# Sparse mixture-of-experts block: weight low halves moved between GpSimd and VectorE

## The chip, the cores and the metric

One core of a Trainium2 chip runs the whole kernel in one launch. The metric is device time in microseconds (us) of that core. Its engines run their own instruction lists side by side and meet only at semaphores: TensorE (PE in the profile), VectorE (DVE), ScalarE (ACT), GpSimd (POOL) and SyncE (SP, which here only issues DMAs).

## The reference, cut to what matters

```python
x = x + tanh(g_xattn) * xattn(layernorm(x), ctx, mask)      # (2, 1024, 256) tokens x width
h = layernorm(x)                                            # 2048 tokens
top_logits, top_idx = top_k(h @ w_router, 2)                # 8 experts, two for each token
moe = sum over the two chosen experts e of
      score_e * ((silu(proj_e) * gate_e) @ fc2_w[e])        # proj_e, gate_e = split(h @ fc1_w[e])
shared = (silu(h @ gate_w) * (h @ up_w)) @ down_w           # 512 wide, for every token
x = x + tanh(g_ffn) * (moe + shared)
```

## The kernel before, in words

All matmuls that need full float32 accuracy are done in three passes: each operand is split into a high half (the value rounded to the matmul's type) and a low half (what is left). For the weights, ScalarE writes the high halves (`cut_hi`) and `cut_lo` writes the low halves as `raw - high`, one 128x512 chunk at a time, on GpSimd or on VectorE. There are 30 chunks: 0 to 5 belong to the shared part, 6 to 29 to the experts (three for each). The split by engine is by hand: `by_pool(i)` is true for the chunks before `IN_A` (7), for those in `MID` and for those in `LAST` (27, 28, 29); these are GpSimd's. All others are VectorE's.

The stages that matter here, in order of time:

1. The shared part of the FFN runs on TensorE in 16 units (4 groups of 512 tokens by 4 slices of 128). From unit 4 on, `gate_up_down(n, n - 2)` interleaves gate and up of unit n with the down product of unit n - 2. VectorE serves each unit with `product(n)` (L690 or L692), then `cut_later(n)`, which cuts `LATER[n]` of VectorE's own chunks (L243), then `product_lo(n)` (L630), the low half of the unit's activations. The down product of unit n needs `product_lo(n)`. Units 14 and 15 are held back for the end of the kernel.
2. Meanwhile GpSimd scatters the 2048 normalised token rows to the two experts of each, into the DRAM buffer `rows`: 32 indirect DMAs of 128 rows (L388), 16 for each half of the tokens, `scatter(h, n0, n1)`. The low halves of `MID` stand between them by hand, those of `LAST` behind the last scatter.
3. When all scatters have landed, SyncE loads the 39 expert tiles of 128 rows each (`hrows<-rows`, L281). TensorE transposes tile 0 (L1245), does `down(12)`, transposes tile 1, and waits for all weight low halves before the first expert matmul `m_up(0)` (L994).
4. The loop over the 39 tiles, then the two units held back, and the sums.

TensorE's own order at the seam of stages 1 and 3 is `gate_up(13)`, `down(11)`, `m_turn_x(0)`, `down(12)`, `m_turn_x(1)`, `m_up(0)`. `down(n)` and `product_lo(n)` meet at this wait:

```python
            def down(n):
                g, f = n // FC, n % FC
                after(pe, "chunk_lp", SCH)
                after(pe, "act_l", n + 1)
```

On VectorE the same place reads `product(12)`, three low halves, `product_lo(12)`, `product(13)`, `m_x(0)`.

Of the kernel before, what the change touches and what calls it, by code (L numbers as in the profile page):

```python
# [44 lines left out]
HT = NT // NH  # L45
IN_A = 7
HELD = 2
U0 = UNITS - HELD
MID = tuple(IN_A + 2 * i for i in range(5))
LAST = tuple(range(CHUNKS - 3, CHUNKS))  # L50
LATER = {3: 1, 4: 1, 5: 1, 6: 1, 7: 1, 8: 1, 9: 2, 10: 2, 11: 2, 12: 3}
ORDER = list(range(SCH + 8)) + list(range(SCH + 12, CHUNKS)) + list(range(SCH + 8, SCH + 12))


def build(nc, x, ctx_t, ctx_in, mask, small, W_t, chunks, out):
# [6 lines left out]
    with ExitStack() as ctx:  # L62
# [149 lines left out]
        def after(eng, name, value):  # L212
            if not (isinstance(value, int) and value <= 0):
                eng.wait_ge(s[name], value)
# [13 lines left out]
        def chunk_bufs(i):  # L228
            c = ORDER[i]
            raw_, hi_, lo_ = (sw_raw, sw_hi, sw_lo) if c < SCH else (ew_raw, ew_hi, ew_lo)  # L230
            c = c if c < SCH else c - SCH
            return raw_[:, c, :], hi_[:, c, :], lo_[:, c, :]

        def by_pool(i):
            return i < IN_A or i in MID + LAST

# [3 lines left out]
        def cut_lo(eng, i):  # L240
            after(eng, "chunk_h", i + 1)
            raw_, hi_, lo_ = chunk_bufs(i)
            eng.tensor_tensor(out=lo_, in0=raw_, in1=hi_.bitcast(F32), op=ALU.subtract)\  # L243
                .then_inc(s["chunk_lp" if by_pool(i) else "chunk_lv"], 1)
# [60 lines left out]
        def _(pool):  # L305
# [64 lines left out]
            def weight_fields(h):  # L370
                sl = slice(HT * h, HT * h + HT)
                after(pool, "tg_half", 2)
                after(pool, "w_tanh", h + 1)
                pool.tensor_scalar(hrows[:, sl, D + 2], wsm[:, 3, sl], tgh[:, 0:1], tgh[:, 0:1], ALU.mult, ALU.add)\
                    .then_inc(s["fields"], 1)
                pool.tensor_scalar(hrows[:, sl, D + 3], wsm[:, 3, sl], tgh[:, 1:2], None, ALU.mult)\
                    .then_inc(s["fields"], 1)

            def scatter(h, n0, n1):
                if n0 == 0:  # L380
                    after(pool, "h_ready", HT * (h + 1))
                    after(pool, "fields", 2 * (h + 1))
                    after(pool, "low_expert", h + 1)
                    after(pool, "const_r", 6)
                    after(pool, "slots", h + 1)
                for n in range(n0, n1):
                    k, i = n % 2, n // 2
                    pool.indirect_dma_start(  # L388
                        out=rows, out_offset=bass.IndirectOffsetOnAxis(ap=slot[:, h, k, i:i + 1], axis=0),
                        in_=hrows[:, HT * h + i, :], in_offset=None, bounds_check=PAD_ROW - 1, oob_is_err=False,  # L390
                    ).then_inc(s["scattered"], 16)
# [20 lines left out]
            rstd_second(NG - 1)  # L412
            scatter(0, 3, 8)
            cut_lo(pool, MID[0])
            scatter(0, 8, 12)
            cut_lo(pool, MID[1])
            scatter(0, 12, 2 * HT)
            cut_lo(pool, MID[2])
            weight_fields(1)
            scatter(1, 0, 6)  # L420
            cut_lo(pool, MID[3])
            scatter(1, 6, 11)
            cut_lo(pool, MID[4])
            scatter(1, 11, 2 * HT)
            for i in LAST:
                cut_lo(pool, i)
            for t in range(N_TILES):
# [198 lines left out]
        def _(v):  # L626
# [163 lines left out]
            def cut_later(u):  # L790
                mine = [i for i in range(IN_A, CHUNKS) if i not in MID + LAST]
                first = sum(m for w, m in LATER.items() if w < u)
                for i in mine[first:first + LATER.get(u, 0)]:
                    cut_lo(v, i)
# [557 lines left out]
```

## Time and profile before

| what | value |
|---|---|
| median of 3 runs | 240.39 us |
| the three runs | 238.53, 250.59 and 240.39 us |
| span of the profiled execution, first to last instruction | 237.5 us |
| TensorE busy in it | 222.3 us (94%) |
| VectorE busy | 171.8 us (72%) |
| GpSimd busy | 125.1 us (53%) |
| ScalarE busy | 129.8 us (55%) |
| granted TensorE clock, mean | 0.998 |

The total time of the profiled execution is not given apart from its span; the quickest of the three runs is 1.03 us longer than the span. Busy shares are averages over all stages. The kernel's stages have different limits, so the rows below are taken from the stretch from 70 to 122 us, in which the scatters run and the expert tiles begin.

### The profile page before, as it was taken

To read this page: it belongs to the slowest core of one execution; us is meant where nothing else is said; L and a number is where in the kernel's file an instruction comes from. 1 tells how busy PE (TensorE), PEld (TensorE's weight loads), DVE (VectorE), ACT (ScalarE), POOL (GpSimd) and SP (SyncE) were. 2 spreads that over 40 slices of the span, in tenths; PEclk is the share of its full clock that TensorE was granted. 3 is DMA by queue.
4 is the path that set the end of the run, shared out by engine and by line. 5 is a ranking of instruction groups with operands and counts; after the bars stand their busy time and mean duration, and the time that the engine had idled before them with its cause. 6 is when DMAs were issued, how large, how long until landed. Compare 5 with 4: busy or idle time off the path is not lost.

```text
span 237.5 us, 5283 instructions
## 1 busy us (share of the span) xinstructions
PE 222.3 (94%) x1425; PEld 193.7 (82%) x1425; DVE 171.8 (72%) x513; ACT 129.8 (55%) x316; POOL 125.1 (53%) x177
## 2 busy tenths in 40 slices
PE   7688999999989999999599999999999999999984
PEld 7578999978778888888488888888888888888763
DVE  0977897797767799999977665665665665664794
ACT  2465788773647645464125656656656656655320
POOL 1688898464777887887701334334334334334600
PEclk9999999999999999999999999999999999999999
DMA  5999950000121225322242443343343332008877
GB/s 154 286 362 406 404 199 3 0 0 25 45 94 67 74 85 179 136 91 92 67 123 65 135 127 94 96 125 96 88 127 92 94 120 68 37 38 267 288 238 310
DMA packets 18131, 32.05 MB, mean 135 GB/s; under 512 B 3046, under 2 KB 9323, under 8 KB 18104
## 3 DMA queue, kind: packets, MB, share of 16 engines
q1 hardware_dynamic: 14096, 22.28, 29.8%
q0 software_dynamic: 3408, 8.46, 9.5%
q10 hardware_dynamic: 600, 0.97, 1.3%
q8 instruction: 13, 0.21, 0.4%
q14 instruction: 14, 0.11, 0.2%
HBM read 19.95 MB, written 12.67 MB: 137 GB/s over the span
## 4 chain that ended last, share of the span: by engine, by line
PE 46%; POOL 8%; issue 6%; DMA 2%; DVE 2%; SPq 0%; DVEq 0%; ACT 0%; POOLq 0%
PE bank L994 38%; POOL rows L388 6%; PE bank L1245 4%; PE bank L1265 3%; POOL ew_lo L243 2%; DMA rows<-hrows,slot 1%; DMA hrows<-rows 1%; DVE act_lo L630 1%; DVE acc L710 0%; PE bank L1179 0%; DVE act L929 0%; DVE acc L966 0%; SPq L280 0%; ACT act L581 0%; DVEq L62 0%
## 5 line engine op out<-in xcount | busy, mean ns | idle before, releaser
L430 POOL DMA_INDIRECT parts<-y_out,dst x39 | 38.7, 991 | 69.9 <-DVE dst L923 66.1
L388 POOL DMA_INDIRECT rows<-hrows,slot x32 | 35.0, 1095 | 12.3 <-issue 12.3
L929 DVE TENSOR_TENSOR act<-act,bank 128x256 f32<-128x256 f32 x39 | 16.4, 421 | 34.5 <-issue 25.0
L581 ACT ACTIVATE act<-bank 128x256 f32<-128x256 f32 x39 | 15.0, 384 | 37.1 <-PE bank L994 37.1
L994 PE MATMUL bank<-ew_hi,m_xt_hi 128*128 x78 | 30.9, 396 | 0.1
L994 PE MATMUL bank<-ew_hi,m_xt_lo 128*128 x78 | 30.8, 395 | 0.0
L994 PE MATMUL bank<-ew_lo,m_xt_hi 128*128 x78 | 30.7, 394 | 0.0
L994 PE MATMUL bank<-ew_hi,act_hi 128*128 x78 | 25.2, 323 | 0.1
L994 PE MATMUL bank<-ew_hi,act_lo 128*128 x78 | 21.9, 281 | 0.0
L994 PE MATMUL bank<-ew_lo,act_hi 128*128 x78 | 21.9, 281 | 0.0
L443 ACT ACTIVATE act_hi<-act 128x512 fp32r<-128x512 f32 x16 | 10.1, 630 | 21.2 <-DVE act L690 9.1
L593 ACT ACTIVATE y_out<-bank,w_t 128x256 f32<-128x256 f32 x39 | 18.5, 475 | 4.0 <-PE bank L994 1.1
L443 ACT ACTIVATE m_xt_hi<-bank 128x256 fp32r<-128x256 f32 x39 | 14.9, 381 | 5.8 <-PE bank L1245 5.8
L630 DVE TENSOR_TENSOR act_lo<-bank,act_hi 128x256 fp32r<-128x256 f32 x39 | 16.5, 423 | 1.6 <-ACT act_hi L443 1.0
L994 PEld LDWEIGHTS bank<-ew_hi,m_xt_lo 128*128 128x128 f32 x78 | 14.7, 188 | 3.3
L1245 PEld LDWEIGHTS bank<-ident,hrows 128*128 128x128 f32 x78 | 10.7, 140 | 8.0 <-issue 3.1
L1245 PE MATMUL bank<-ident,hrows 128*128 128x128 f32 x78 | 14.9, 272 | 2.5 <-DMA hrows<-rows 2.5
L994 PEld LDWEIGHTS bank<-ew_hi,m_xt_hi 128*128 128x128 f32 x78 | 14.7, 188 | 2.2 <-issue 0.4
L630 DVE TENSOR_TENSOR m_xt_lo<-bank,m_xt_hi 128x256 fp32r<-128x256 f32 x39 | 16.1, 414 | 0.4 <-ACT m_xt_hi L443 0.4
L443 ACT ACTIVATE act_hi<-bank 128x256 fp32r<-128x256 f32 x39 | 15.0, 384 | 2.6 <-PE bank L1265 0.6
L994 PEld LDWEIGHTS bank<-ew_lo,m_xt_hi 128*128 128x128 f32 x78 | 14.7, 188 | 1.8
L243 DVE TENSOR_TENSOR ew_lo<-ew_raw,ew_hi 128x512 fp32r<-128x512 f32 x15 | 15.6, 1037 | 0.2
(186 smaller groups left out, 655.6 us busy)
## 6 DMA issues: line engine op xcount, KB each, us to landing
ew_raw<-in_chunks SPq DMA_DIRECT2D x12, 512.0 KB, 10.7
hrows<-rows SPq DMA_DIRECT2D x39, 130.0 KB, 2.1
low_buf<-parts SPq DMA_DIRECT2D x4, 512.0 KB, 4.6
high_buf<-parts SPq DMA_DIRECT2D x4, 512.0 KB, 3.9
acc<-in_x SPq DMA_DIRECT2D x7, 256.0 KB, 4.6
sw_raw<-in_chunks SPq DMA_DIRECT2D x3, 512.0 KB, 9.0
out<-acc SPq DMA_DIRECT2D x3, 512.0 KB, 3.0
rows<-pad_rows SPq DMA_DIRECT2D x9, 130.0 KB
```

Source lines behind the costliest of these rows:

```text
L243: eng.tensor_tensor(out=lo_, in0=raw_, in1=hi_.bitcast(F32), op=ALU.subtract)\
L388: pool.indirect_dma_start(out=rows, out_offset=bass.IndirectOffsetOnAxis(ap=slot[:, h, k, i:i + 1], axis=0), in_=hrows[:, HT * h + i, :], ...
L430: pool.indirect_dma_start(out=parts, out_offset=bass.IndirectOffsetOnAxis(ap=dst[:, t:t + 1], axis=0), in_=y_out[:, t % SLOTS, :], in_offs ...
L443: return a.activation(out_, in_, ACT.Identity).then_inc(s[name], 1)
L581: a.activation(act[:, p, 0:I], M_H[p][:, 0:I], ACT.Silu).then_inc(s["m_sil"], 1)
L593: a.activation(y_out[:, t % SLOTS, :], M_Y[p][:, 0:D], ACT.Identity, scale=w_t[:, t:t + 1])\
L630: return TT(out_, in_, hi_.bitcast(F32), ALU.subtract).then_inc(s[name], 1)
L929: TT(act[:, p, 0:I], act[:, p, 0:I], M_H[p][:, I:2 * I], ALU.mult).then_inc(s["m_prod"], 1)
L994: ins = pe.matmul(ps, a, b, start=first and i == 0, stop=last and i == total - 1, skip_group_check=not lone)
L1245: ins = pe.transpose(M_X[:, k * P:(k + 1) * P], hrows[:, i, k * P:(k + 1) * P], ident[:])
L1265: ins = pe.transpose(M_A[:, k * P:(k + 1) * P], act[:, p, k * P:(k + 1) * P], ident[:])
```

## The change

Chunks 9 and 15 go from GpSimd to VectorE. The scatters, which stood in series of 5, 4, 4, 6, 5 and 5 between the low halves of the list, now stand in series of 5, 8, 8 and 8. VectorE's list of chunks gets chunk 9 in unit 4 and chunk 15 (by its place in the list, 16 and 17 stand there) in unit 8: each of the two units cuts one more.

```diff
-MID = tuple(IN_A + 2 * i for i in range(5))
+MID = (IN_A, IN_A + 4, IN_A + 6)
-LATER = {3: 1, 4: 1, 5: 1, 6: 1, 7: 1, 8: 1, 9: 2, 10: 2, 11: 2, 12: 3}
+LATER = {3: 1, 4: 2, 5: 1, 6: 1, 7: 1, 8: 2, 9: 2, 10: 2, 11: 2, 12: 3}
@@ on GpSimd
             cut_lo(pool, MID[0])
-            scatter(0, 8, 12)
+            scatter(0, 8, 2 * HT)
             cut_lo(pool, MID[1])
-            scatter(0, 12, 2 * HT)
+            weight_fields(1)
+            scatter(1, 0, 8)
             cut_lo(pool, MID[2])
-            weight_fields(1)
-            scatter(1, 0, 6)
-            cut_lo(pool, MID[3])
-            scatter(1, 6, 11)
-            cut_lo(pool, MID[4])
-            scatter(1, 11, 2 * HT)
+            scatter(1, 8, 2 * HT)
             for i in LAST:
                 cut_lo(pool, i)
```

GpSimd before, from the fourth scatter of the first half of the tokens to its last low half; L388 is a scatter, L243 a low half, L374 and L376 write the routing weights of the second half:

```order
L388 DMA rows<-hrows,slot 17536x260 x5
L243 TENSOR_TENSOR ew_lo<-ew_raw,ew_hi 128x512
L388 DMA rows<-hrows,slot 17536x260 x4
L243 TENSOR_TENSOR ew_lo<-ew_raw,ew_hi 128x512
L388 DMA rows<-hrows,slot 17536x260 x4
L243 TENSOR_TENSOR ew_lo<-ew_raw,ew_hi 128x512
L374 TENSOR_SCALAR hrows<-wsm,tgh 128x8
L376 TENSOR_SCALAR hrows<-wsm,tgh 128x8
L388 DMA rows<-hrows,slot 17536x260 x6
L243 TENSOR_TENSOR ew_lo<-ew_raw,ew_hi 128x512
L388 DMA rows<-hrows,slot 17536x260 x5
L243 TENSOR_TENSOR ew_lo<-ew_raw,ew_hi 128x512
```

Behind these, five more scatters and the three low halves of `LAST` follow. The same place in the changed kernel:

```order
L388 DMA rows<-hrows,slot 17536x260 x5
L243 TENSOR_TENSOR ew_lo<-ew_raw,ew_hi 128x512
L388 DMA rows<-hrows,slot 17536x260 x8
L243 TENSOR_TENSOR ew_lo<-ew_raw,ew_hi 128x512
L374 TENSOR_SCALAR hrows<-wsm,tgh 128x8
L376 TENSOR_SCALAR hrows<-wsm,tgh 128x8
L388 DMA rows<-hrows,slot 17536x260 x8
L243 TENSOR_TENSOR ew_lo<-ew_raw,ew_hi 128x512
L388 DMA rows<-hrows,slot 17536x260 x8
L243 TENSOR_TENSOR ew_lo<-ew_raw,ew_hi 128x512 x3
```

Two low halves are gone from between the scatters, and nothing else on GpSimd has changed its order.

VectorE before, in unit 8: `product(8)`, its low half of weights, `product_lo(8)`, `product(9)`:

```order
L904 CAST t_off<-t_offf 128x39
L690 TENSOR_TENSOR act<-act,bank 128x512
L243 TENSOR_TENSOR ew_lo<-ew_raw,ew_hi 128x512
L630 TENSOR_TENSOR act_lo<-act,act_hi 128x512
L690 TENSOR_TENSOR act<-act,bank 128x512
```

And in the changed kernel, whose lines are numbered four lower from here on:

```order
L900 CAST t_off<-t_offf 128x39
L686 TENSOR_TENSOR act<-act,bank 128x512
L243 TENSOR_TENSOR ew_lo<-ew_raw,ew_hi 128x512 x2
L626 TENSOR_TENSOR act_lo<-act,act_hi 128x512
L686 TENSOR_TENSOR act<-act,bank 128x512
```

One low half more stands ahead of the activations' low half. The other added one stands in unit 4, behind `product(4)` and ahead of the slots of the second half (`place`, L783 before). The orders of TensorE, ScalarE and SyncE are the same.

## Rows read from the trace of the kernel before

**Rows 1.** The page, part 1: busy us (share of the span) xinstructions

```profile
PE 222.3 (94%) x1425; PEld 193.7 (82%) x1425; DVE 171.8 (72%) x513; ACT 129.8 (55%) x316; POOL 125.1 (53%) x177
```

**Rows 2.** The chain of waits at the seam: start us, us, what

```profile
111.64 0.30 issue
111.95 2.90 DMA rows<-hrows,slot
...
115.66 2.14 DMA hrows<-rows
117.79 0.14 issue
117.93 0.41 PE bank L1245 x2
118.34 0.17 issue
118.51 1.67 PE bank L994 x12
```

**Rows 3.** GpSimd's timeline: start us, us, instruction [idle before <-releaser]

```profile
73.51 1.00 POOL L388 DMA_INDIRECT rows<-hrows,slot  x1 [0.16 <-issue]
...
76.14 0.97 POOL L388 DMA_INDIRECT rows<-hrows,slot  x1 [0.30 <-issue]
77.41 1.30 POOL L388 DMA_INDIRECT rows<-hrows,slot  x1 [0.31 <-issue]
78.72 1.31 POOL L243 TENSOR_TENSOR ew_lo<-ew_raw,ew_hi 128x512 fp32r<-128x512 f32 x1
80.20 0.99 POOL L388 DMA_INDIRECT rows<-hrows,slot  x1 [0.17 <-issue]
...
87.96 1.08 POOL L388 DMA_INDIRECT rows<-hrows,slot  x1 [0.85 <-issue]
...
93.55 1.49 POOL L388 DMA_INDIRECT rows<-hrows,slot  x1 [0.30 <-issue]
95.35 0.97 POOL L388 DMA_INDIRECT rows<-hrows,slot  x1 [0.30 <-issue]
96.34 1.30 POOL L243 TENSOR_TENSOR ew_lo<-ew_raw,ew_hi 128x512 fp32r<-128x512 f32 x1
...
104.81 1.32 POOL L243 TENSOR_TENSOR ew_lo<-ew_raw,ew_hi 128x512 fp32r<-128x512 f32 x1
...
111.95 1.39 POOL L388 DMA_INDIRECT rows<-hrows,slot  x1 [0.30 <-issue]
113.35 3.77 POOL L243 TENSOR_TENSOR ew_lo<-ew_raw,ew_hi 128x512 fp32r<-128x512 f32 x3
```

**Rows 4.** GpSimd's groups, 86 to 114 us: xcount | busy us, mean ns | idle before

```profile
L388 POOL DMA_INDIRECT rows<-hrows,slot x16 | 18.4, 1152 | 5.1 <-issue 5.1
```

**Rows 5.** VectorE's timeline, 77 to 119 us

```profile
77.18 0.68 DVE L243 TENSOR_TENSOR ew_lo<-ew_raw,ew_hi 128x512 fp32r<-128x512 f32 x1
79.42 0.23 DVE L783 TENSOR_TENSOR place<-bank,e_reg 128x64 f32<-128x64 f32 x1 [1.55 <-PE bank L1091]
...
96.50 1.19 DVE L904 CAST t_off<-t_offf 128x39 int32<-128x39 f32 x1
...
99.04 0.69 DVE L630 TENSOR_TENSOR act_lo<-act,act_hi 128x512 fp32r<-128x512 f32 x1 [0.15 <-issue]
...
104.47 2.95 DVE L243 TENSOR_TENSOR ew_lo<-ew_raw,ew_hi 128x512 fp32r<-128x512 f32 x2
...
111.14 0.75 DVE L692 SCALAR_TENSOR_TENSOR act<-act,tg,bank 128x512 f32<-128x512 f32 x1 [0.35 <-PE bank L1144]
111.81 5.87 DVE L243 TENSOR_TENSOR ew_lo<-ew_raw,ew_hi 128x512 fp32r<-128x512 f32 x3
117.71 0.69 DVE L630 TENSOR_TENSOR act_lo<-act,act_hi 128x512 fp32r<-128x512 f32 x1
```

**Rows 6.** TensorE's timeline: unit 10 begins, and the seam

```profile
99.88 0.41 PE L1144 MATMUL bank<-ht_hi,sw_hi 128*128 128x512 f32 x1
...
115.19 0.28 PE L994 MATMUL bank<-sw_hi,act_lo 128*128 128x256 f32 x1
117.93 0.41 PE L1245 MATMUL bank<-ident,hrows 128*128 128x128 f32 x2 [2.46 <-DMA hrows<-rows]
```

## The prediction

> **What bounds the kernel now.** I read the busy shares first: TensorE is busy 94% of the span [rows 1], so a change on GpSimd and VectorE can only pay where TensorE waits. The chain of waits then names the place. From about 84 us to 112 us it runs over GpSimd's scatters, then over the landing of the last scatter, the load of the first expert tile and its transpose [rows 2]. TensorE's timeline shows what that costs: the last matmul of `down(11)` ends at 115.47 us, and the transpose of tile 0 starts at 117.93, an idle time of 2.46 us ended by the tile's load [rows 6]. That is all this seam can give back at the transposes, however early the scatters end.
>
> The reader should look at one more line of the chain: between the transposes (end 118.34) and `down(12)` (start 118.51) there are 0.17 us put down to nothing [rows 2]. `down(12)` needs `product_lo(12)`, and on VectorE this one runs from 117.71 to 118.40 [rows 5]. So two things come last together: the tile's load and VectorE's low half of activations. The chain shows only the first. Why VectorE is so late stands in its timeline: the three weight low halves of unit 12 take 5.87 us [rows 5], while one low half takes 0.68 [rows 5]. The excess, 5.87 - 3 x 0.70 = 3.77 us, is exactly the time of GpSimd's three `LAST` low halves, 113.35 to 117.12 [rows 3]. VectorE's third low half ends at 117.68, 0.56 us behind GpSimd's end. The same is seen at 104.47, where two of VectorE's take 2.95 us beside one of GpSimd's from 104.81 to 106.13, and at 96.50, where a small cast takes 1.19 us and ends 0.05 us behind GpSimd's low half [rows 3, 5]. `product(12)` reads PSUM and took a plain 0.75 us, but nothing in that row is a test, since GpSimd was at a scatter then. In this trace GpSimd's low half runs its 1.3 us whatever VectorE does, and VectorE's operation on SBUF waits for it.
>
> **Part 1: two low halves leave GpSimd's list.** Scatters in a quiet stretch start 1.27 us apart (76.14 to 77.41) [rows 3]. With a low half between, it costs its own 1.31 us plus 0.17 of gap behind it, and saves the 0.30 gap between two scatters: 1.31 + 0.17 - 0.30 = 1.18 us. Two of them: 2.36 us off the path that ends at 113.35.
>
> **Part 2: what the moved work does to the scatters.** A scatter beside VectorE work is often longer than its 0.97: the 16 of the second half of the tokens take 18.4 us [rows 4], 18.4 - 16 x 0.97 = 2.9 us over. Single ones are 1.30 beside a VectorE low half at 77.18, 1.39 beside those at 111.81, 1.49 at 93.55 [rows 3, 5]. One more VectorE low half in unit 4 and one in unit 8 may therefore stretch one scatter each, by 0 (many scatters show none) to 0.52 (1.49 - 0.97). I take 0.18 each, the mean of the 16 (2.9 / 16): 0.36 us. GpSimd's scatters then end 2.36 - 0.36 = 2.0 us earlier, at 111.35; the bounds are 2.36 - 1.04 = 1.3 and 2.36. The row is no floor for the stretch either: the second half's 2.9 us could come out smaller by chance of how the two lists meet. That is rival two.
>
> By the Trainium skill (SBUF — State Buffer, Who interferes with whom) a VectorE operation with two SBUF inputs contends with a GpSimd instruction that reads SBUF, while descriptor generation, which is what a scatter does on GpSimd, was not stalled by `tensor_tensor`. The stretched scatters in this trace (1.30 and 1.39 against 0.97, both beside such low halves) speak against the second half of that. By the page the end would move by the whole 2.36, and the result below would be 0.96 instead of 0.6.
>
> **Part 3: VectorE's own time.** In unit 4 the added 0.68 us lies in the 1.55 us in which VectorE waits for the rank matmuls [rows 5]: nothing, and if that cover were gone, 0.7 us of a list that has 1.5 us in hand. In unit 8 VectorE has no idle time to speak of; `product_lo(8)` runs at 99.04 to 99.73 and TensorE's up of unit 10 needs it at 99.88 [rows 5, 6]. GpSimd's one remaining low half of this stretch comes later than the one at 96.34: the second half starts at about 86.8 (87.96 less 1.18), and eight scatters at 25.4 / 16, less the two low halves between them (23.0 / 16 = 1.44 us each), end at 98.3. So it meets the two low halves of unit 8, where it costs VectorE some 1.1 us, and the cast at 96.50 saves its 1.1. Net, `product_lo(8)` is 0.7 to 1.1 us late, and TensorE waits about as long, less the 0.15 in hand. The wait at 104.81 (1.5 us of VectorE) disappears afterwards. TensorE carries a delay of 0.5 to 1.0 us to the end of `down(11)`, 116.0 to 116.5, where it used to sit idle until 117.93. So it costs nothing now; without that idle time it would be the whole 0.5 to 1.0.
>
> **Part 4: the seam.** The load follows the scatters: 117.79 - 2.0 = 115.8, transpose possible at 115.9, so from there the start could be 118.51 - 2.0 = 116.5 for `down(12)`. But GpSimd's `LAST` now runs from 111.35 to 115.12, and `product(12)` ends at 111.8 or later. Before, VectorE had finished two of its three low halves ahead of `LAST`; now all three wait. They end 0.56 + 2 x 0.70 = 1.96 us behind GpSimd, and `product_lo(12)` 0.72 later: 115.12 + 1.96 + 0.72 = 117.8 against 118.40. The gain is GpSimd's gain less two low halves: 2.0 - 1.40 = 0.6 us. All that follows (`product(13)`, `m_x(0)`, transpose 1, `m_up(0)`) hangs on VectorE and TensorE in the same distances and moves by the same 0.6; from there TensorE is continuous and the rest keeps its length. The bounds of part 2 give 1.3 - 1.4 = -0.1 and 2.36 - 1.4 = 0.96, so 0 to 1.0.
>
> **The sum.** The profiled span would go from 237.5 to 236.9 us. With the 1.0 us that the quickest run has over the span, that is 237.9, beside the quickest run of 238.53. The median of the runs, 240.39, lies 2.9 over the span. I apply the same difference to the median: 240.39 - 0.6 = 239.8 us. A measurement of this kernel can tell about 2% (4.8 us) from no change; the whole idle time at the seam is half of that.
>
> **Rivals.** *One, the full idle time is recovered* (chance 0.13). If VectorE's low halves of unit 12 got ahead of `LAST`, or were not held by it, `down(12)` would follow TensorE's own list: 118.51 - 2.46 = 116.05, or 116.9 with part 3's delay. That is a gain of 1.6 to 2.46 us, 237.9 to 238.8. For it: VectorE's held low half at 104.47 is recorded as begun before GpSimd's. Against it: all collisions in the rows ended with VectorE behind GpSimd. The Trainium skill (SBUF — State Buffer, Who interferes with whom) says that the one that starts first keeps the port for its instruction; taken with the recorded starts, the trace disagrees.
>
> *Two, the scatters speed up more than by the two low halves* (chance 0.1): if the 2.9 us of stretch shrank to half, they would end 1.5 us earlier still, and the gain would be 0.6 + 1.5 = 2.1 us, 238.3. The quiet series around 80 us speaks for it, VectorE's steady load up to 111 us against it.
>
> *Three, slower: the unbroken series themselves are slower* (chance 0.2). No series in the rows is longer than six. The fifth of one series, at 93.55, has 1.80 us to the next start at 95.35, 0.53 over the quiet step. If GpSimd fell back to such steps from the seventh scatter of each series of eight on, that is 3 x 2 x 0.53 = 3.2 us more, against 2.0 less: scatters end 1.2 us later. `LAST` then starts behind VectorE's low halves, so the tile's load alone sets the seam and the kernel is 1.2 us slower, 241.6. It decides from 0.33 us for each of the six scatters on. What speaks against it is that the long steps stand as well inside short series and beside VectorE work.
>
> *Four, slower: VectorE runs behind* (chance 0.07). Two low halves at 0.7 and one more collision of 1.3 would be 2.7 us, against TensorE's 2.46 of idle time: 0.3 us slower, 240.7.
>
> **How the numbers follow.** The forecast (0 to 1 us quicker) has 0.5, the rivals 0.13, 0.1, 0.2 and 0.07. The mechanisms reach from 237.9 to 241.6 on the median. The three runs of before differ among themselves by more, 238.53 to 250.59, and a median over few runs may sit at the quick end: 238.53 - 2.1 = 236.4. The range is 236.6 to 242.0. None of the cases passes 2% by itself; only the spread of the runs can. Hence 0.04 for faster by over 2%, 0.92 for within, 0.04 for slower.
>
> **What would show it.** In the profile of the changed kernel: the last scatter starts at about 110 and `LAST` at about 111.4; VectorE's three low halves of unit 12 take some 5.3 us and end about 2 us behind `LAST`; TensorE has a wait of 0.5 to 1.0 us in unit 10, a transpose of tile 0 around 116.3, and a new idle time of about 1.2 us ahead of `down(12)`, ended by VectorE and no longer by the load. If `LAST` starts near 113, part 1 or part 2 is wrong; if `down(12)` starts before 117, part 4 is.

## Result, and the profile after

| | median, us | quickest to slowest, runs |
|---|---|---|
| before | 240.25 | 238.53 to 250.59, 4 |
| changed | 246.81 | 242.28 to 249.15, 4 |

The ratio is 1.0166, with a 95% interval of 1.0111 to 1.0221: slower, though whether by more than 2% is not settled, and the median lies outside the range of 236.6 to 242.0. In every set of this document the ratio leaves out executions over 1.5% above the quickest of the same kernel (here 249.15 and 248.27 of the changed one and 250.59 of before), so this one compares two executions with three and is nearer to 1 than the two medians are. The profiled execution of the changed kernel is the one of 249.15 us, with a span of 247.4 us against 237.5; it shows the loss at its largest. Lines of the changed kernel are numbered four lower than those of before.

Page of the changed kernel, parts 1 and 2:

```profile
PE 229.1 (93%) x1425; PEld 197.7 (80%) x1425; DVE 166.5 (67%) x515; ACT 130.0 (53%) x316; POOL 120.4 (49%) x175
PEclk9999999999999999985799999999999999999999
```

VectorE and GpSimd did less than before [rows 1], TensorE more: its clock is down in three slices of 6.2 us. GpSimd's timeline (start us, us, instruction, idle before):

```profile
77.33 1.31 POOL L388 DMA_INDIRECT rows<-hrows,slot  x1 [0.30 <-issue]
...
83.77 1.31 POOL L243 TENSOR_TENSOR ew_lo<-ew_raw,ew_hi 128x512 fp32r<-128x512 f32 x1
...
86.54 1.08 POOL L388 DMA_INDIRECT rows<-hrows,slot  x1 [0.85 <-issue]
...
96.82 1.30 POOL L243 TENSOR_TENSOR ew_lo<-ew_raw,ew_hi 128x512 fp32r<-128x512 f32 x1
98.28 1.26 POOL L388 DMA_INDIRECT rows<-hrows,slot  x1 [0.17 <-issue]
...
107.72 0.97 POOL L388 DMA_INDIRECT rows<-hrows,slot  x1 [0.30 <-issue]
```

The scatters are not the loss. The last one ends at 108.69, where it ended at 113.34 before [rows 3]: 4.65 us earlier, against the 2.0 of the forecast. The series did what rival two said, not what rival three said. Now VectorE (same columns):

```profile
80.82 0.23 DVE L779 TENSOR_TENSOR place<-bank,e_reg 128x64 f32<-128x64 f32 x1 [2.30 <-remote]
...
85.22 0.69 DVE L686 TENSOR_TENSOR act<-act,bank 128x512 f32<-128x512 f32 x1 [2.65 <-remote]
...
102.00 0.69 DVE L686 TENSOR_TENSOR act<-act,bank 128x512 f32<-128x512 f32 x1 [0.82 <-PE bank L1140]
102.61 1.41 DVE L243 TENSOR_TENSOR ew_lo<-ew_raw,ew_hi 128x512 fp32r<-128x512 f32 x2
104.05 0.69 DVE L626 TENSOR_TENSOR act_lo<-act,act_hi 128x512 fp32r<-128x512 f32 x1
110.00 0.69 DVE L686 TENSOR_TENSOR act<-act,bank 128x512 f32<-128x512 f32 x1 [5.25 <-remote]
110.60 1.65 DVE L702 SCALAR_TENSOR_TENSOR acc<-bank,tg,acc 128x256 f32<-128x256 f32 x4
```

`product(5)` at 85.22 and `product(9)` at 110.00 each wait for the up product of their unit. The profile puts both waits down to "remote", an unknown releaser. On one core there is no other core; the name appears because TensorE's records say that the product had been done long before: the last up matmul of unit 5 ends at 81.2, that of unit 9 at 101.6. VectorE has no wait of this name between 60 and 130 us of the kernel before; `place` waited 1.55 us there, for the rank matmuls [rows 5]. VectorE's waits between 70 and 130 us of the changed kernel (what waited for what: us in total, times, longest):

```profile
DVE act L686 <- remote: 7.9, 2, 5.3
DVE act L686 <- PE bank L1140: 3.4, 2, 2.6
DVE place L779 <- remote: 2.3, 1, 2.3
```

TensorE itself does not run late at first; it then runs out of banks and operands, since VectorE cannot go on. Its two waits in unit 11:

```profile
110.83 0.77 PE L1126 MATMUL bank<-ht_hi,sw_hi 128*128 128x512 f32 x1 [1.98 <-DVE act L686]
...
114.36 0.80 PE L1140 MATMUL bank<-ht_hi,sw_hi 128*128 128x512 f32 x1 [0.63 <-DVE act_lo L626]
```

Busy time by stretch in the changed kernel: us, then TensorE, its weight loads, VectorE, ScalarE, GpSimd (each with its instructions), the granted clock, and the DMA engines' busy share and GB/s.

```profile
104.00:108.00 4.00, 3.66 (x20) 2.45 (x18) 0.71 (x2) 1.64 (x3) 3.09 (x4) 1.00 0.33 116
108.00:112.00 4.00, 1.60 (x5) 1.19 (x5) 2.00 (x5) 1.28 (x3) 0.69 (x1) 0.74 0.19 66
112.00:116.00 4.00, 3.37 (x10) 2.26 (x9) 3.90 (x7) 1.93 (x5) 0.00 (x0) 0.50 0.48 133
116.00:120.00 4.00, 4.00 (x16) 3.60 (x15) 1.40 (x3) 1.09 (x3) 1.27 (x1) 0.50 0.45 113
```

VectorE is idle for 3.3 of 4 us from 104 on, TensorE then for 2.4 of the 4 us from 108 on, and in that second stretch its clock goes from 1.00 to 0.50 (0.74 on average), that is from 2.4 to 1.2 GHz. It stays there to 120 us: from 112 to 120 TensorE does 26 matmuls with 0.63 us of idle time, where it does 56 in a run with the full clock (chip A, below).

**Where a product's completion goes.** The trace also holds the semaphore events, by which TensorE tells the others that a product is done. I set the time of the event beside the recorded end of the product's last matmul. Not every event is in the trace; where one is missing, the start of the step that waited for it shows which product an event belongs to (`product(9)` starts at 110.00, so up(9) was told at 109.9).

| product | before: done, told | changed, profiled execution: done, told |
|---|---|---|
| gate(5), and the rank matmuls beside it | 78.6, 79.3 | 78.5, 80.7 |
| up(5) | 81.4, 81.4 | 81.2, 85.1 |
| gate(8) | 91.3, 92.2 | 93.3, 98.1 |
| up(8) | 93.9, 96.7 | 95.9, 101.9 |
| gate(9) | 95.5, 96.8 | 97.6, 104.9 |
| up(9) | 98.1, (not in the trace) | 101.6, 109.9 |
| gate(10) | 100.0, 100.1 | 104.5, 110.0 |

The events do not come late by a constant. They come in bursts: three products are told from 85.12 to 85.24 and three from 109.90 to 110.02, each time 1.2 to 1.4 us after the end of a series of scatters on GpSimd (83.75, 108.69). At a pause they catch up, wholly or in part (of what was pending at the pause from 96.80 us only gate(8) is told, at 98.15), and in the next series they fall behind again. In the trace of before the same is seen twice, smaller: 0.7 us at gate(5), in the series of four that ends at 78.71, and up to 2.8 us in its only series of six (87.96 to 96.32). How far TensorE's units end behind those of before shows the loss building up: 2.0 us in unit 8, 3.5 in unit 9 and 6.0 in unit 10 by held completions, then 12.8 in unit 11. Of these last 6.8 us, 2.6 are TensorE's two waits for VectorE (1.98 and 0.63), and most of the rest is the clock. The 2.46 us of idle time at the seam [rows 6] take up most of what separates 12.8 from the final 9.9.

### The profile page after: what moved, and what is told of

Its sections match the earlier page's. It is cut to its first block, busy times and chain, and to the rows that moved or that the text cites. A ratio compares the mean times of both kernels' runs of the same rounds, so it can differ in the third digit from the quotient of the medians.

```text
span 247.4 us, 5285 instructions
## 1 busy us (share of the span) xinstructions
PE 229.1 (93%) x1425; PEld 197.7 (80%) x1425; DVE 166.5 (67%) x515; ACT 130.0 (53%) x316; POOL 120.4 (49%) x175
## 4 chain that ended last, share of the span: by engine, by line
PE 71%; DVE 10%; issue 5%; another core or an unknown queue 4%; POOL 3%; ACT 3%; DMA 2%; DVEq 0%; POOLq 0%; ACTq 0%
PE bank L990 45%; PE bank L1140 4%; PE bank L1241 4%; PE bank L1261 3%; PE bank L1147 3%; PE bank L1024 3%; PE bank L1036 2%; DVE ew_lo L243 2%; DMA acc<-in_x 2%; PE bank L1126 2%; DVE act_lo L626 2%; PE bank L1064 1%; DVE acc L702 1%; PE bank L1074 1%
## 5 line engine op out<-in xcount | busy, mean ns | idle before, releaser
L388 POOL DMA_INDIRECT rows<-hrows,slot x32 | 32.8, 1026 | 12.6 <-issue 12.6
L686 DVE TENSOR_TENSOR act<-act,bank 128x512 f32<-128x512 f32 x12 | 8.2, 684 | 14.4 <-remote 7.9
L243 POOL TENSOR_TENSOR ew_lo<-ew_raw,ew_hi 128x512 fp32r<-128x512 f32 x7 | 9.0, 1294 | 13.5 <-ACT ew_hi L439 12.7
L1261 PE MATMUL bank<-ident,act 128*128 128x128 f32 x78 | 14.9, 273 | 0.4 <-DVE act_lo L626 0.4
```

What stands on the lines that cost most here:

```text
L388: pool.indirect_dma_start(out=rows, out_offset=bass.IndirectOffsetOnAxis(ap=slot[:, h, k, i:i + 1], axis=0), in_=hrows[:, HT * h + i, :], ...
L1261: ins = pe.transpose(M_A[:, k * P:(k + 1) * P], act[:, p, k * P:(k + 1) * P], ident[:])
```

## Experiments

The runs fall into five sets, each on another chip (called A to E), with at least 23 executions of the kernel before in each. Each kernel of a set has one profiled execution (the kernel before only in the first set), and all times at which a product is told come from it. In the expectations, S is the theory that long unbroken series hold back what TensorE has finished, and V that VectorE's own added work makes the loss; C is that the chip or the moment of the first set counts, M that two series with too little pause between them run into one.

**Chip A, the change again.**

> The changed kernel unchanged, to see whether its loss is of the kernel or of single executions. Its profile had TensorE's completions reaching VectorE and ScalarE late (product(9) waited 5.25 us), not a GpSimd or VectorE list that is longer. Theory S (unbroken series of scatters hold back TensorE's completions): 242 to 247 us again, 1 to 3% over the kernel before, with waits of 2 us and more on VectorE in units 5 to 10. Theory C (chance: such delays hit any execution): back to within 0.5% of the kernel before. Theory V (two more low halves on VectorE): as S in time, but with VectorE busy when TensorE waits.

Measured: 239.59 us (238.78 to 241.78, 12 executions), ratio 0.9992 [0.9971, 1.0013]. The loss of the first set is gone, but the held completion is not, at least in the profiled execution, which is the longest of the twelve (241.78 us). VectorE's timeline and waits in it:

```profile
85.04 0.69 DVE L686 TENSOR_TENSOR act<-act,bank 128x512 f32<-128x512 f32 x1 [3.22 <-remote]
```

```profile
DVE act L686 <- remote: 3.2, 1, 3.2
```

up(5) is done at 81.4 and told at 84.94; gate(8) is 0.9 late and up(8) 2.7 (told at 98.42). All that was pending is told in the pause from 97.3 to 98.8 us, and the last series starts clean. In the first set it did not, and there the two traces part.

**The series alone.** Five low halves stay on GpSimd and VectorE's list is as before; only the places change.

```diff
-            scatter(0, 8, 12)
+            scatter(0, 8, 2 * HT)
             cut_lo(pool, MID[1])
-            scatter(0, 12, 2 * HT)
             cut_lo(pool, MID[2])
             weight_fields(1)
-            scatter(1, 0, 6)
+            scatter(1, 0, 8)
             cut_lo(pool, MID[3])
-            scatter(1, 6, 11)
+            scatter(1, 8, 2 * HT)
             cut_lo(pool, MID[4])
-            scatter(1, 11, 2 * HT)
```

> The kernel before with all five low halves on GpSimd and VectorE's list as before; only their places change: the scatters stand in series of eight, with the low halves behind them (two behind the first half's last scatter, one behind the last scatter of all, so the last scatter ends about 1.2 us earlier). Theory S: slower than before by 1 to 3%, late completions as in the changed kernel. Theory V and theory C: within 0.5% of before, or some tenths quicker.

Measured: 241.64 us (6), 1.0103 [1.0063, 1.0144]: moving low halves on GpSimd makes the kernel slower, though its work is the same. up(5) is told at 84.33 and up(8) at 98.85, 3.6 and 3.7 us late.

```profile
DVE act L688 <- remote: 3.3, 1, 3.3
DVE place L781 <- PE bank L1089: 2.2, 1, 2.2
```

Not all of the 1% need be the series. Run late by the waits, VectorE comes to `product_lo(11)` only when GpSimd begins the low halves behind its last scatter, here four of them and not three, and is held by them:

```profile
110.85 5.05 POOL L243 TENSOR_TENSOR ew_lo<-ew_raw,ew_hi 128x512 fp32r<-128x512 f32 x4
```

```profile
110.75 5.70 DVE L628 TENSOR_TENSOR act_lo<-act,act_hi 128x512 fp32r<-128x512 f32 x1
```

How much the fourth adds was not run apart; one low half is some 1.3 us.

**VectorE's list alone.** The changed lists, with a subtraction of a 128x512 array from itself (a stand-in that writes an unused buffer) at the two places that lost a low half.

```diff
-LATER = {3: 1, 4: 1, 5: 1, 6: 1, 7: 1, 8: 1, 9: 2, 10: 2, 11: 2, 12: 3}
+LATER = {3: 1, 4: 2, 5: 1, 6: 1, 7: 1, 8: 2, 9: 2, 10: 2, 11: 2, 12: 3}
...
+                pool.tensor_tensor(out=scrap[:], in0=same, in1=same, op=ALU.subtract).then_inc(s["scrap"], 1)
```

> The changed kernel with two stand-in operations on GpSimd of the same size (128x512, both inputs in SBUF, output to a scratch tile) where the two low halves used to be: GpSimd's list is the one before in kind, place and length (series of 5, 4, 4, 6, 5, 5), VectorE's list is the changed one. Theory V: as slow as the changed kernel, 1 to 3%. Theory S: as the kernel before, at most 0.7 us more. Theory C: as before.

Measured: 240.47 us (12), 1.003 [1.0003, 1.0058]. VectorE's added work with the pauses kept costs 0.7 us (0.1 to 1.4). up(5) is told on time at 80.94, and its waits between 70 and 90 us have no "remote":

```profile
DVE act L696 <- PE bank L1000: 1.2, 1, 1.2
DVE place L789 <- PE bank L1097: 0.8, 1, 0.8
```

V is out as the cause of the held completion of unit 5. up(8) is 2.8 us late here, behind the series of six, as in the kernel before.

**A short break.** The changed kernel, with a one-column `memset` behind the 12th and the 27th scatter and its third low half back behind the 22nd, so that the series are those of before.

```diff
-            scatter(0, 8, 2 * HT)
+            scatter(0, 8, 12)
+            pool.memset(scrap[:, 0:1], 0.0).then_inc(s["scrap"], 1)
+            scatter(0, 12, 2 * HT)
```

> The changed kernel, its two long series cut again at the old places by a memset of one column on GpSimd (some 0.1 us in place of 1.3). If what matters is that a series is broken at all, this is as quick as before or 0.6 us quicker. If what matters is GpSimd's free time between scatters, or how many scatters fall into a stretch of time, it is as slow as the changed kernel (1 to 3% over before). Theory V: as slow as the changed kernel.

Measured: 240.25 us (12), 1.0028 [1.001, 1.0046]. GpSimd's timeline and VectorE's waits:

```profile
102.50 0.12 POOL L424 MEMSET scrap<- 128x1 f32 x1
102.81 1.15 POOL L389 DMA_INDIRECT rows<-hrows,slot  x1 [0.19 <-issue]
```

```profile
DVE act L691 <- remote: 4.2, 2, 3.2
```

A break of 0.12 us does nothing: up(5) is told at 84.66, 3.5 us late. The `memset` fits into the 0.30 us that lie between any two scatters: the one behind the 12th scatter (77.08 to 78.38) is followed by the next at 78.69, 0.31 later. So it did not lengthen the pause, and what counts would be GpSimd's time away from scatters; the kind of instruction, which differs too, was not varied by itself.

**Chip B, the change a third time.**

> The changed kernel a third time, unchanged. First it took 1.7% more than the kernel before, the second time 0.1% less. If the loss belongs to the chip or the hour and not to the kernel, the ratio lies anywhere between 0.999 and 1.02, with every execution of the set on one side; if the second set is the rule, 0.997 to 1.003. In the profile the up product of unit 5 (due at 81.5 us) should reach VectorE at about 85 us in either case, as in both profiles so far.

Measured: 239.70 us (12), 0.9988 [0.9966, 1.0011], and the same 3.2 us of "remote" in front of `product(5)`, as on chip A (in an execution of 240.22 us, the second longest of the twelve).

**Four low halves, well spaced.** One low half fewer on GpSimd than before, and series of 5, 4, 4, 5, 5 and 6.

```diff
-MID = tuple(IN_A + 2 * i for i in range(5))
+MID = tuple(IN_A + 2 * i for i in range(4))
-LATER = {3: 1, 4: 1, 5: 1, 6: 1, 7: 1, 8: 1, 9: 2, 10: 2, 11: 2, 12: 3}
+LATER = {3: 1, 4: 2, 5: 1, 6: 1, 7: 1, 8: 1, 9: 2, 10: 2, 11: 2, 12: 3}
             scatter(0, 12, 2 * HT)
-            cut_lo(pool, MID[2])
             weight_fields(1)
-            scatter(1, 0, 6)
+            scatter(1, 0, 5)
+            cut_lo(pool, MID[2])
+            scatter(1, 5, 10)
             cut_lo(pool, MID[3])
-            scatter(1, 6, 11)
-            cut_lo(pool, MID[4])
-            scatter(1, 11, 2 * HT)
+            scatter(1, 10, 2 * HT)
```

> Four low halves stay among the scatters and one (chunk 15) goes to VectorE, in unit 4; series of 5, 4, 4, 5, 5, 6, so none is longer than before and the break ahead of the second half is GpSimd's two small operations alone. Theory S (completions of TensorE are held back in long unbroken series): no late completion in unit 5, scatters end 1.2 us earlier than before, time 0.3 to 1.2 us under the kernel before (ratio 0.995 to 0.999). Theory V (more VectorE work in unit 4 costs): slower than before by 0.3 us or more.

Measured: 238.28 us (237.80 to 239.50, 11), 0.993 [0.9908, 0.9953]. This is more than the 0.995 to 0.999 that was expected, and why is open: 1.7 us quicker than before with one low half off GpSimd, where the change takes off two and gets 0.2 to 1.2 on chips A, B, D and E. up(5) is told at 80.81, on time. In its series of five up(7) is still 1.9 us late (89.18, told at 91.11), and VectorE waits for it:

```profile
DVE act L689 <- remote: 1.2, 1, 1.2
```

**Half a pause.** The changed kernel with stand-ins of 128x256 (0.63 us) at the two places.

> As e3_vector_alone, with stand-ins of half the width (128x256, some 0.6 us in place of 1.1). How long must the break be? A break of 0.12 us left the completion of unit 5 3.3 us late, one of 1.1 us left it on time. If the held-back completions drain in proportion to the break, it comes out between, late by 1 to 2 us; if any break over some tenths is enough, on time. The result's output is complete, since the stand-ins write a scratch tile only.

Measured: 240.13 us (12), 1.0009 [0.9984, 1.0035]. up(5) is on time (80.86). The stand-in leaves 0.82 us between its two scatters, and that suffices there where 0.31 did not; VectorE's waits from 70 to 90 us:

```profile
DVE act L696 <- PE bank L1000: 1.2, 1, 1.2
```

**One long series.** The kernel before, with only the first half's low half moved from between scatters 12 and 13 to behind 16, which makes one series of eight.

> The kernel before with one series of eight only, in the first half of the tokens (the low half behind its twelfth scatter moves behind its sixteenth); GpSimd's work and VectorE's list are as before. Theory S: up of unit 5 is 3 to 4 us late, VectorE waits for it some 3 us, and the whole is 0.5 to 1.5 us slower than before. Otherwise no difference at all.

Measured: 241.05 us (12), 1.0044 [1.0016, 1.0072]. up(5) is told at 84.92:

```profile
DVE act L689 <- remote: 3.2, 1, 3.2
DVE place L782 <- PE bank L1090: 2.2, 1, 2.2
```

One moved instruction brings the wait of 3.2 us, with nothing taken off or added. Together with the series alone and with the two runs with stand-ins, this shows S for this place, on chips A and B. It shows as well how the wait becomes a loss: `product_lo(11)`, at 110.10 in the kernel before and clear of `LAST` there, now meets `LAST` (112.49 to 116.30).

```profile
112.40 4.46 DVE L629 TENSOR_TENSOR act_lo<-act,act_hi 128x512 fp32r<-128x512 f32 x1
```

**Chip C, the change a fourth time.**

> The changed kernel unchanged, for one more set of executions: if the loss of the first set was of that set alone, 0.997 to 1.003 of the kernel before; if it comes back on some chips, 1.01 to 1.02 with all executions over 242 us.

Measured: 246.84, 240.31, 246.69 and 246.08 us; there is no ratio for it. None of the 29 executions of the kernel before on this chip took over 241.51. This is the first set's loss again, and its picture too (VectorE's waits):

```profile
DVE act L686 <- remote: 8.1, 2, 5.4
DVE place L779 <- remote: 2.3, 1, 2.3
```

up(9) is done at 100.9 and told at 108.44. GpSimd's last scatter starts at 106.85, the earliest of all runs.

**Low halves behind the activations.** In unit 12 `cut_later` moves behind `product_lo`, in the spaced kernel and in the kernel before.

```diff
-                cut_later(u)
+                if u < U0 - 2:
+                    cut_later(u)
                 product_lo(u)
+            cut_later(U0 - 2)
```

> e6_four_spaced with VectorE's three low halves of unit 12 behind product_lo(12) in place of ahead of it. Theory of the prediction's part 4 (down(12) waits for product_lo(12), which stands behind low halves held by GpSimd's LAST): down(12) starts 1 to 2 us earlier, but m_up(0) still waits for all low halves, which end about 2 us behind LAST; time 0 to 0.8 us under e6_four_spaced, at about 237.5 to 238.3 us. Rival (the tile's load sets the seam alone): no difference from e6_four_spaced.

> The kernel before with the same reordering alone. There the load of tile 0 ends at 117.79 us whatever VectorE does, so down(12) can start at most 0.17 us earlier; and the three low halves, now behind product_lo(12), delay product(13) and with it the rest: 0.997 to 1.006 of the kernel before, most likely within 0.3%.

Measured: 238.98 us (237.94 to 240.34, 12), 0.9971 [0.9944, 0.9998], and 241.03 (12), 1.0036 [1.0002, 1.0069]. No gain over before in the second; the first stays under before, by less than the spaced kernel did on chip B (0.993), so no gain is seen there either, though the two were not run side by side. TensorE's waits in the second:

```profile
PE bank L1247 <- DMA hrows<-rows: 1.9, 1, 1.9
PE bank L1247 <- DVE m_xt_lo L630: 1.3, 1, 1.3
```

The wait of `down(12)` has moved to the next step that needs VectorE, the low half of tile 0. For the long executions the first of the two counts more: on the chip on which three of four executions of the changed kernel took 246 us, none of the twelve of this spaced one took over 240.34.

**Less work on VectorE.** In units 5 to 9 the low halves that VectorE cuts are written as zero, by an operation with one input; part of the weights' accuracy is left out.

```diff
+                    if 5 <= u <= 9:
+                        after(v, "chunk_h", i + 1)
+                        TS(chunk_bufs(i)[2], chunk_bufs(i)[1].bitcast(F32), 0.0, None, ALU.mult).then_inc(s["chunk_lv"], 1)
```

> The changed kernel in which the seven low halves that VectorE cuts in units 5 to 9 are set to zero instead (one multiplication by zero with one input, in place of a subtraction with two), so that part of the weights' accuracy is left out. It asks where a held-back completion leads when VectorE disturbs the scatters less. Theory F (VectorE's two-input operations stretch scatters, and the stretch is what lets TensorE's completions drain; in the slow first execution the scatters of the second half ran at the bare 0.97 us, 13 of 16): scatters of 0.97 to 1.0 us, completions in units 8 and 9 later than 4.5 us, time 241 us and more. Theory without feedback: scatters and completions as in the other profiles of the changed kernel, time 238 to 239.5 us because VectorE has less to do.

Measured: 241.85 us (10), 1.0071 [1.0032, 1.011], two executions at 246.36 and 248.66. Even with less to do VectorE stood waiting, 4.1 us for "remote". It speaks once more against VectorE's load as the cause. Of the feedback theory it bears out one half: 12 of the 16 scatters of the second half took 0.97 to 0.98 us and the time was over 241, but the completions of units 8 and 9 were 2.7 us late at most (up(8)), where over 4.5 was expected. Why this chip fell behind further stays open.

**Chip D, the change a fifth time.**

> The changed kernel unchanged, beside the next three on one chip. So far its executions fall into two groups, 24 of 24 at 238.8 to 241.8 us in two sets, and 6 of 8 at 245 to 249 in the two others. Either group may be met here; it tells which of the next three runs can be read for the slow group.

Measured: 238.72 us (238.04 to 239.93, 12), 0.9953 [0.9932, 0.9974]. Here not one completion was held in the profiled execution, in the same series of eight: up(5) is done at 80.90 and told at 80.92, up(8) at 93.48 and 93.50. The run is the test of the prediction's other steps, below.

**Longer pause between the last two series**: two stand-ins of 128x512 behind `cut_lo(pool, MID[2])`.

> The changed kernel with two stand-ins more (2.1 us) in GpSimd's pause between its last two series of eight, 3.4 us of pause in place of 1.3. In the slow executions only 8 of the 16 arrivals of the scatter before that pause were recorded in it, and the last two series ran on as one, with completions up to 8 us late. Theory M (the slow group is the one in which that pause is too short to drain): no execution over 244 us even where e13 has them, at the price of scatters that end 2.1 us later than its fast ones (240 to 242.5 us). Otherwise: as many executions of 245 us and more as e13.

Measured: 242.05 us (10), 1.0077 [1.0052, 1.0102]. Beside the changed kernel of the same set this is some 3 us more (242.05 against 238.72); `LAST` starts 2.5 us later (113.61 against 111.11). With no completion held on this chip, whether the pause would help is untested.

**The spaced kernel again, and the first series alone cut.**

> e6_four_spaced unchanged, on another chip: 0.990 to 0.996 of the kernel before, none of its executions over 241 us. If the slow group belongs to the chip and not to the long series, it has such executions too wherever e13 has them.

> The changed kernel with one stand-in behind the twelfth scatter of the first half; the two series of eight of the second half stay. Unit 5's completion on time. If the slow group starts from the first long series, none of its executions is over 244 us; if the two series of the second half suffice, it has the slow group wherever e13 has it. Where e13 is in its fast group: within 0.4% of the kernel before.

Measured: 238.40 us (238.15 to 239.30, 12), 0.9942 [0.9915, 0.9968], and 239.23 (12), 0.9976 [0.9955, 0.9998]. The spaced kernel repeats its gain over before. It is not clear of the changed kernel on this chip (0.9953 [0.9932, 0.9974]), and the 0.5 us that the stand-in behind the 12th scatter seems to cost is within the noise too.

**Chip E, the change and the longer pause again.**

> The changed kernel unchanged, once more beside the kernel with the longer pause. Four sets of executions had it at 0.995 to 0.999 or at 246 us, by the chip. Which of the two comes here is not foreseen.

> e14_longer_pause unchanged. Theory M (too short a pause between the last two series of eight makes the slow group): no execution over 244 us even if e17 has them, 1.005 to 1.010 of the kernel before. Otherwise the same share of executions over 245 us as e17.

Measured: 238.34 us (12), 0.9952 [0.9929, 0.9976], and 241.34 (12), 1.0058 [1.0025, 1.0091]. As on chip D, no "remote" wait, and no answer on M.

**The six sets of the changed kernel**, side by side:

| set | ratio to before | longest "remote" wait | arrivals of the 32 scatters in the trace, of 512 |
|---|---|---|---|
| first | 1.0166 [1.0111, 1.0221] | 5.3 us | 174 |
| A | 0.9992 [0.9971, 1.0013] | 3.2 us | 207 |
| B | 0.9988 [0.9966, 1.0011] | 3.2 us | 199 |
| C | none; median 246.38 of 4 | 5.4 us | 177 |
| D | 0.9953 [0.9932, 0.9974] | none | 512 |
| E | 0.9952 [0.9929, 0.9976] | none | 510 |

The kernel before stays at 239.75 to 239.88 us on all five chips. The time of the changed kernel goes with how long its completions are held, each time in one profiled execution.

The last column counts semaphore events: each scatter signals 16 arrivals. It parts the chips in the same way, and not for the changed kernel alone. In all fourteen traces of the first set and of chips A, B and C, the kernel before (253 arrivals) and the spaced ones included, over half of these arrivals and 66 to 74 of TensorE's 272 events are missing; in all six of chips D and E at most 4 arrivals and 5 of TensorE's events are. So completions were held only on chips where the trace itself loses events. Which of the two brings the other, or whether a third thing brings both, is not shown.

## Why the prediction was wrong

**The step that failed** is part 3: "TensorE waits about as long, less the 0.15 in hand", and "So it costs nothing now". With it goes rival three. All my prices for TensorE came from VectorE's list: how late `product_lo(8)` would be. The runs show a cost that no term held. On four of six occasions a product of TensorE is told 3.5 to 3.9 us late in a series of eight scatters, and where the second half's two series run into one, up to 8.3 us late. The idle time of 2.46 us, meant to take up 0.5 to 1.0 us, can take up the first, which left TensorE 1.8 us behind in unit 8 on chip A (gate(8) ends at 93.1 against 91.3), and not the second. Rival three named the right place, "the unbroken series themselves", and the wrong victim: it let GpSimd's scatters grow longer (1.2 us in all, 241.6), while in the first set they ran quicker, and TensorE and VectorE paid. The range took its upper end from that rival and so left out the executions of 246 us and more.

The trace of before held the sign. In its series of six from 87.96 us on, up(8) is done at 93.9 and told at 96.69; and 0.7 of the 1.55 us of `place`, which part 3 took for time of the rank matmuls, is their completion told late (78.7, 79.3). I read durations and waits, and never set the time of a completion beside the end of its matmul.

**The rest can be read where nothing was held**, on chip D. No profile of the kernel before was taken on it, so the times are set beside those of [rows 2] to [rows 6]. In both, gate(4) is done ahead of anything that the change touches, and on chip D that is already 0.45 us earlier (73.00 against 73.45). GpSimd, VectorE and TensorE there, one fence each:

```profile
98.42 1.32 POOL L243 TENSOR_TENSOR ew_lo<-ew_raw,ew_hi 128x512 fp32r<-128x512 f32 x1
...
111.11 3.81 POOL L243 TENSOR_TENSOR ew_lo<-ew_raw,ew_hi 128x512 fp32r<-128x512 f32 x3
```

```profile
98.20 2.10 DVE L626 TENSOR_TENSOR act_lo<-act,act_hi 128x512 fp32r<-128x512 f32 x1
...
112.39 4.54 DVE L243 TENSOR_TENSOR ew_lo<-ew_raw,ew_hi 128x512 fp32r<-128x512 f32 x3
116.97 0.69 DVE L626 TENSOR_TENSOR act_lo<-act,act_hi 128x512 fp32r<-128x512 f32 x1
```

```profile
100.36 0.50 PE L1140 MATMUL bank<-ht_hi,sw_hi 128*128 128x512 f32 x1 [1.07 <-DVE act_lo L626]
...
116.41 0.41 PE L1241 MATMUL bank<-ident,hrows 128*128 128x128 f32 x2 [0.36 <-DMA hrows<-rows]
117.76 0.36 PE L990 MATMUL bank<-sw_hi,act_hi 128*128 128x256 f32 x1 [0.94 <-issue]
```

- *Parts 1 and 2, GpSimd:* the low half meets VectorE at 98.42 (forecast 98.3), `LAST` starts at 111.11 (111.35, from 113.35 before [rows 3]). Right; less the 0.45 us, the scatters end some 0.2 us later than forecast. The 16 scatters of the second half take 18.2 us, against 18.4 [rows 4].
- *Part 3, TensorE's delay:* one wait of 1.1 us for `product_lo` in unit 10 (forecast 0.5 to 1.0; the low half of GpSimd holds `product_lo(8)` itself, not the two low halves ahead of it), and `down(11)` ends at 116.05 (116.0 to 116.5). About right where no completion is held.
- *Part 4, the seam:* the three low halves end 2.0 us behind `LAST` (1.96), the transpose is at 116.41 (116.3), a new idle time of 0.94 stands ahead of `down(12)` (1.2), which starts at 117.76 (117.8, from 118.51 [rows 2]). The step held: of the 2.36 us taken off GpSimd only 0.75 reach `down(12)`, and 0.3 without the head start of 0.45, since VectorE's low halves now queue behind `LAST`.
- *The sum:* 0.47% of 239.9 is 1.1 us (0.6 to 1.6), where 0.6 was forecast (0 to 1.0). The forecast is inside that interval, and the medians are better evidence than the times of single steps above, in which luck of 0.45 us is as large as what is sought.
- *Rival one* (VectorE's low halves get ahead, full idle time recovered) is out: they ended behind `LAST` in every profile, and moving them by hand (the reordered kernels) brings nothing, as the next step on VectorE is held instead.
- *Rival two* came true in the first set, 4.65 us earlier, with the gain eaten by the waits. *Rival four* is out as the cause of the loss: VectorE's added work costs 0.3% (0.7 us) with the pauses kept, and on chips D and E, with it, the changed kernel is quicker than before.

**Shown, and open.** Shown is that series of eight bring late completions and a loss on chips A and B (series alone 1.0103, in part perhaps by its fourth low half at the end; one series 1.0044), that stand-ins of 0.63 us or more there bring up(5) back on time, and that the spaced kernel is quicker than before (0.993 and 0.994 in two sets). That the loss of the first set is the same thing grown larger rests on its trace and on that of chip C: same waits, same bursts; no run varied the kernel on a chip while it showed the loss side by side, except that on chip C none of twelve executions of the spaced and reordered kernel was over 240.34. Not shown is a feedback: in those two the scatters of the second half mostly take a bare 0.97 us (10 to 12 of 16), as if VectorE, starved, stretched none, and the series run together; but with 12 of 16 bare the run with less work on VectorE was not held longer, and a run on chip E (the longer pause) held nothing. Open is what holds the completions (the path of the semaphores, or the writing of the profiler's own records; both are on in every execution here, so that the whole loss may be one of profiled executions), why chips D and E, whose traces are nearly complete, show nothing of it, and whether a longer pause between the last two series would have saved the first set.

## What to carry to other kernels

When short instructions stand between indirect DMAs on GpSimd, treat them as pauses before removing them: here series of up to six with a low half or a stand-in of at least 0.6 us between them held completions for 3 us at most, and the kernel with the shorter series was the quickest, while series of eight held them for 3.5 us and more in four sets of six. In a trace, set the time at which a semaphore is raised beside the end of what raises it; a wait for an unknown releaser on a kernel of one core was the sign here that these had come apart. Count the events in the trace too, against what the program signals: where many are missing, the profile and perhaps the run itself are disturbed. Repeat a change like this on several chips, since the same kernel stood at 0.995, 0.999 and 1.017 of before.

## What the runs showed of the hardware

- With scatters of 128 rows starting every 1.28 us on GpSimd without a break, TensorE's completions reached VectorE 3.5 to 3.9 us late after some eight of them, and up to 8.3 us late (up(9), 101.6 to 109.9) after 16 with one pause that didn't clear the backlog. This was so in the first set and on chips A, B and C. A `memset` of 0.12 us in between did not help, a stand-in of 0.63 us did. On chips D and E the same series held nothing (up(5) told 0.02 us after its end).
- In the stretches with late completions the events of the scatters' own landings are scarce too: of the 16 arrivals that a scatter signals, mostly 0 to 6 are in the trace for those inside a series, and all 16 for the one before most pauses. At the pause from 96.80 us of the first set, and at the same one on chip C, only 8 of 16 were there, on chips A and B all 16. On chips D and E all but a few are there, inside a series too (512 and 510 of 512).
- The records' own path would fit. The Trainium skill says that the internal pipeline of the block that writes them holds up its producers rather than lose a record (NOTIFIC — the notification-queue block, 7.1 Overflow). No run here shows it. That 66 to 74 of TensorE's 272 events are missing where completions are held, and at most 5 where none is, fits a choked path of records, but not the words that nothing is lost, unless the loss lies outside that block. It was not tried, as the profiler's records can't be separated from the run.
- VectorE's operation with two SBUF inputs waited for all of GpSimd's low halves in a row, not for one: 5.70 us beside four (5.05 us, series alone), 4.46 us beside three (3.81 us, one series), against 0.69 by itself, though each was recorded as begun 0.09 to 0.10 us ahead of GpSimd's.
- TensorE's granted clock fell from 1.00 to 0.50 in the stretch in which it was busy for 1.60 of 4 us (108 to 112 us of the first set), and a 512-column matmul went from 0.40 to 0.63 us; and the delay of 6.0 us became 12.8 within one unit.
